# Rearranging the first forty microseconds of a four-layer recurrent kernel on one core

## What is computed

```
h = x_norm @ Win.T + bin
for each of 4 layers:
    y = silu(layernorm(h));  y = sconv(y)      # complex decaying recurrence along the tokens
    h = h + y * scl
    y = silu(layernorm(h) @ W1.T + b1) @ W2.T + b2
    h = h + y
x = x + layernorm(layernorm(h) @ Wout.T + bout)
```

## Time and profile before

| | |
|---|---|
| median of three timed runs | 204.45 us (204.21 to 204.62) |
| profiled execution | 204.57 us, of it the span 202.8 us |
| PE busy | 181.9 us, 90% of the span |
| DVE busy | 157.4 us, 78% |
| ACT, POOL busy | 109.8 us, 84.0 us |
| bytes moved | 15.31 MB, most of them in the first 31 us |

### The profile page before, as it was taken

One profiled execution on the slowest core, in us unless ns is written; L12 is line 12 of the kernel. 1 busy time (PEld: TensorE's weight loads), 2 busy tenths in 40 slices (PEclk: granted clock), 3 DMA queues, 4 the chain that ended last, 5 costly groups with the idle time before them and its releaser, 6 DMA issues.

```text
span 202.8 us, 3759 instructions
## 1 busy us (share of the span) xinstructions
PE 181.9 (90%) x1210; PEld 148.8 (73%) x1210; DVE 157.4 (78%) x547; ACT 109.8 (54%) x281; POOL 84.0 (41%) x142
## 2 busy tenths in 40 slices
PE   0797996859999998999999899999999898988992
PEld 0797995758988788788998689989988444555430
DVE  6898978886588768784977776655899997998872
ACT  1595687524456467637555445462836585863210
POOL 4222269724044422343224522467462735555400
PEclk9999999978999999999999999999999999999999
DMA  5999990000000000000000000000000000002675
GB/s 158 419 376 400 417 368 14 5 0 0 0 5 0 0 3 0 0 3 0 0 0 5 0 0 0 3 0 3 2 0 2 0 3 0 2 0 105 228 283 216
DMA packets 5505, 15.31 MB, mean 75 GB/s; under 512 B 925, under 2 KB 1965, under 8 KB 4462
## 3 DMA queue, kind: packets, MB, share of 16 engines
q1 hardware_dynamic: 5486, 15.07, 19.7%
HBM read 10.87 MB, written 4.19 MB: 74 GB/s over the span
## 4 chain that ended last, share of the span: by engine, by line
PE 68%; DVE 7%; POOL 7%; DMA 6%; ACT 5%; issue 3%; SPq 2%; DVEq 0%; ACTq 0%
PE bank L1508 15%; PE bank L1400 11%; PE bank L1632 7%; PE bank L1490 6%; DMA M<-in_mraw 6%; PE bank L1464 4%; PE bank L1452 4%; POOL RS L360 4%; PE bank L1567 3%; PE bank L1638 3%; POOL M L380 2%; PE bank L1440 2%; PE bank L1556 2%; ACT XA L593 2%; DVE Z L1001 1%
## 5 line engine op out<-in xcount | busy, mean ns | idle before, releaser
L360 POOL TENSOR_TENSOR RS<-SS,nhalf 128x4 f32<-128x4 f32 x36 | 42.9, 1202 | 67.9 <-DVE SS L995 67.6
L1508 PE MATMUL bank<-ffst,HD 128*128 128x128 f32 x256 | 32.7, 283 | 0.0
L1508 PEld LDWEIGHTS bank<-ffst,HD 128*128 128x128 f32 x256 | 31.3, 200 | 0.2
L995 DVE TENSOR_REDUCE SS<-SQ 128x4 f32<-128x260 f32 x36 | 15.2, 421 | 20.9 <-ACT SQ L635 20.3
L1400 PE MATMUL bank<-M,XT 128*128 128x226 f32 x128 | 27.6, 362 | 0.1
L659 ACT ACTIVATE HD<-bank,b1r 128x512 f32<-128x512 f32 x32 | 20.3, 684 | 10.9 <-PE bank L1490 10.8
L1400 PEld LDWEIGHTS bank<-M,XT 128*128 128x128 f32 x128 | 23.2, 189 | 3.6 <-issue 3.1
L635 ACT ACTIVATE SQ<-bank 128x256 f32<-128x256 f32 x36 | 13.8, 383 | 19.6 <-PE bank L1508 9.6
L640 ACT ACTIVATE Y<-bank,cvst 128x512 f32<-128x512 f32 x16 | 12.5, 779 | 15.1 <-PE bank L1452 15.1
L1035 DVE TENSOR_TENSOR_SCAN V<-cvst,U 128x514 f32<-128x514 f32 x16 | 19.5, 1218 | 0.0
L1490 PE MATMUL bank<-Z,w1r 64*128 64x256 f32 x128 | 18.1, 402 | 0.4
(11 more groups left out here) (265 smaller groups left out, 346.0 us busy)
## 6 DMA issues: line engine op xcount, KB each, us to landing
XT<-in_xT SPq DMA_DIRECT2D x4, 1024.0 KB, 11.7
X<-in_x SPq DMA_DIRECT2D x4, 1024.0 KB, 14.0
out<-X SPq DMA_DIRECT2D x8, 512.0 KB, 2.9
w1r<-in_w1d SPq DMA_DIRECT2D x1, 516.0 KB, 16.5
lt<-in_late SPq DMA_DIRECT2D x1, 449.5 KB, 16.3
M<-in_mraw SPq DMA_DIRECT2D x1, 448.0 KB
w2r<-in_w2n SPq DMA_DIRECT2D x1, 256.0 KB, 11.8
winr<-in_win SPq DMA_DIRECT2D x1, 254.0 KB, 2.6
```

What stands on the lines that cost most here:

```text
L360: pool.tensor_tensor(RS[:, g, :], SS[:, g, :], nhalf[:, :], ALU.pow).then_inc(done, 1)
L995: dve.tensor_reduce(SS[:, g, :], SQ[:, g, :, :], AX.X, ALU.add).then_inc(done, 1)
L1508: last = pe.matmul(HK[g][:, j * P:(j + 1) * P], HD[:, u % 2, a, at:at + P], ffst[:, L, a * P:(a + 1) * P], start=False, stop=True, skip_gr ...
```

## The change

Everything in it is an order of work or a wait that follows from one; two things are added. No other arithmetic changes.

1. Added: PE runs 9 matmuls of `ones` by `ones` into a spare bank as soon as `ones` is set, and 3 after the mean of Win. Nothing reads them.
2. SP issues chp first, c6 before the first XT, and w2r behind X of group 2, no longer ahead of M.
3. DVE begins with the polar form (chp) and weaves the rest of it into the preparation of Win.
4. `first_h(0)` follows table level 1, where it followed level 3; levels 2 and 3 and the four levels of layer 0 are spread behind it. All four levels of layer 0, and `first_h(1)`, now stand ahead of `modulate(0)`; `scan(0)` stands behind `sum_squares(1)`, level 4 of layer 1 and `scale_twice(1)`.
5. PE: `turn1(0)` ahead of `mix_columns`; `setup_ffn` behind `column_sums`; `turn1(2)`, `project_x(0)` and `project_x(1)` ahead of `turn2(0)` and `hidden(0)`. The two projections get banks 6 and 7, and `hidden(0)` waits until they are read.
6. ACT and POOL lists of the filling are written out in an order to match. `square(0)` of the second norm stands between tiles 13 and 14 of the squares; on POOL the norm of unit 0's second half stands behind `input_rstd(3)`.
7. The bias of W2 for unit 0 is one float32 matmul of one row, ahead of the products, in place of the split bf16 one behind them. It waits for `b2_mean`; `ffn_splits` moves behind `sum_squares(4)`.
8. `score_rows` is cut in two: two instructions in step 13, the last four (`score_rests`) in step 14, both ahead of that step's `sum_squares`.

The core of the diff:

```
# SP
+ chp; winr; binr; c6; then as before, with w2r behind X of group 2
# POOL
+            def first_steps():
+                norm(0, ss1, rs1)
+                input_rstd(1)
+                norm(1, ss1, rs1)
+                centre_m(0)
+                input_rstd(2)
+                centre_m(1)
+                norm(2, ss1, rs1)
+                centre_m(2)
+                centre_m(3)
+                input_rstd(3)
+                norm(0, ss2, rs2)
+                norm(3, ss1, rs1)
+                norm(1, ss2, rs2)
+                norm(4, ss1, rs1)
+                norm(2, ss2, rs2)
# ACT
+                square(0, (h0_done, 1), sq1)
+                input_mean(1)
+                input_squares(GT, 2 * GT)
+                mix_rows()
+                silu1(0)
+                square(1, (h0_done, 2), sq1)
+                input_mean(2)
+                input_squares(2 * GT, 2 * GT + 2)
+                column_means()
+                input_squares(2 * GT + 2, 3 * GT)
+                silu1(1)
+                ffn_out()
+                square(2, (h0_done, 3), sq1)
+                input_mean(3)
+                input_squares(3 * GT, 3 * GT + 2)
+                square(0, (a1, 1), sq2)
+                input_squares(3 * GT + 2, 4 * GT)
+                silu1(2)
+                x_out(0)
+                square(3, (h0_done, 4), sq1)
+                x_out(1)
+                z_out(0)
+                square(1, (a1, 2), sq2)
+                silu2(0, 0); silu2(0, 1)
+                silu1(3)
+                square(4, (a2, 1), sq1)
+                z_out(1)
...
# DVE, behind input_stats(0)
+                table_level(0, 0, DEPTH)
+                table_level(1, 0, DEPTH)
+                first_h(0)
+                table_level(2, 0, DEPTH)
                 sum_squares(0, sq1, ss1)
+                table_level(3, 0, DEPTH)
                 scale_twice(0)
+                for k in range(4, 8):
+                    table_level(k, 0, 1)
+                first_h(1)
                 modulate(0)
                 sum_squares(1, sq1, ss1)
                 table_level(4, 1, 2)
                 scale_twice(1)
+                scan(0)
+                demodulate(0)
                 modulate(1)
                 first_h(2)
+                sum_squares(2, sq1, ss1)
+                table_level(5, 1, 2)
+                scale_twice(2)
+                scan(1)
+                demodulate(1)
+                sum_squares(0, sq2, ss2)
+                ffn_means()
+                first_h(3)
                 scale(0, rs2, z2)
+                modulate(2)
+                sum_squares(3, sq1, ss1)
+                scale_twice(3)
                 sum_squares(1, sq2, ss2)
+                scan(2)
                 scale(1, rs2, z2)
                 demodulate(2)
                 modulate(3)
                 sum_squares(4, sq1, ss1)
+                ffn_splits()
                 table_level(6, 1, 2)
                 sum_squares(2, sq2, ss2)
...
+                if s == 13:
+                    score_rows()
+                if s == 14:
+                    score_rests()
                 if GROUPS <= s + 1 < STEPS:
                     sum_squares(s + 1, sq1, ss1)
# PE
+            pe.wait_ge(pool_step, 4)
+            warm(9)
...
             last.then_inc(win_mean, 1)
+            warm(3)
...
                 turn1(0)
+                mix_columns()
                 first_h(2)
                 column_sums()
+                setup_ffn()
                 turn1(1)
                 first_h(3)
+                mix_in(0)
+                turn1(2)
+                project_x(0)
+                mix_in(1)
+                project_x(1)
                 turn2(0, 0)
                 hidden(0)
```

More of the change, by code:

```diff
@@ L362, in step @@
             def step(s):
[L363 to L369, removed]
                 if GROUPS <= s + 1 < STEPS:
@@ L495, in mix @@
                 pool.tensor_tensor(out, GX[:, 2:5, a:b], C2[:, :, a:b], ALU.add).then_inc(mix_ready, 1)
-            for s in range(UNITS + 1):
+            first_steps()
+            for s in range(GROUPS, UNITS + 1):
                 step(s)
[L499 to L503, removed]
             cross(0)
@@ L682, in step @@
                     last_z(s)
[L683 to L689, removed]
+                for t in XSTEP.get(s - 1, ()):
+                    x_out(t)
                 if GROUPS <= s + 1 < STEPS:
@@ L850, in link, with mark @@
                 dve.wait_ge(dve_step, chain[0])
+            def mark(ins):
+                chain[0] += 1
+                ins.then_inc(dve_step, 1)
             for q in range(SG):
@@ L1194, in _ @@
             input_stats(0)
-            for k in range(4):
-                table_level(k, 0, DEPTH)
-            first_h(0)
             first_steps()
@@ L1357, in _, with warm @@
         def _(pe):
+            def warm(n):
+                for i in range(n):
+                    pe.matmul(SPARE[:, 0:P], ones[:, :], ones[:, :], start=True, stop=True)
+            pe.wait_ge(pool_step, 4)
+            warm(9)
             pe.wait_ge(pool_step, 9)
@@ L1391, in project_x @@
                 pe.wait_ge(m_done, VC)
-                if t >= 2 and t not in XSECOND:
+                if t < 2:
+                    pe.wait_ge(w2_read, 2)
+                elif t not in XSECOND:
                     pe.wait_ge(xa_read, t)
@@ L1518, in first_steps @@
                 turn1(0)
+                mix_columns()
                 first_h(2)
                 column_sums()
-                mix_in(0)
+                setup_ffn()
                 turn1(1)
                 first_h(3)
+                mix_in(0)
[3 more added lines that the diff above has]
+                project_x(1)
                 turn2(0, 0)
-                mix_in(1)
-                turn1(2)
                 hidden(0)
-                for t in XSTEP[2]:
-                    project_x(t)
             def step(s):
@@ L1648, in _ @@
             first_h(1)
-            mix_columns()
-            setup_ffn()
             first_steps()
```

105 lines of the change are left out of this document (42 added, 63 removed).

## The result

| | before | after |
|---|---|---|
| median of 20 runs each, on one chip | 204.47 us (from 203.32) | 203.75 us (from 201.59) |
| ratio after to before | | 0.9949 [0.9927, 0.9970] |
| profiled execution, of it the span | 204.57, 202.8 us | 203.30, 201.5 us |

The change gains 0.7 us in the median, and 1.0 us by the ratio, where 3.3 were forecast.

What follows compares the result with a forecast made beforehand. PE was taken as the bound behind the filling, so `turn1(4)`'s start decides. Filling -2.2 us (1.3 + 1.84 - 0.8, less 0.15) and score rows -1.1 make -3.3: 201.3 profiled, 201.1 median; likeliest 200.4 to 202.0, overall 199.9 to 203.3.

Steps and rivals of the forecast that it cites:

- The sum: Whole kernel: 2.2 us from the filling and 1.1 from the score rows, 3.3 us less in all.
- So I take the clock as high, gain 1.84.: End of the filling on PE: no empty stretch like 40:42 remains, so the clock stays high, gaining 1.84 us.
- rival A: New filling: the clock falls again in new PE gaps, one fall costing about 1.84 us, giving 203.0; chance 0.2.
- M and XT of group 2 come 0.63 us earlier: Load queue: with w2r behind X of group 2, these loads come 0.63 us earlier, XT landing at 20.3.
- `first_h(0)`, `scale_twice(0)`, the first products: Early filling: `first_h(0)` at 14.27 (was 16.03), `scale_twice(0)` at 17.55 (was 19.30), 32 product instructions in about 3.8 us.
- all the early gains end in a tie: PE to 32 us: work ends at 31.95, about 31.7 before, since the loads and `setup_ffn` take the early gains.
- `turn1(3)` at 41.35: Late filling on PE: `turn1(3)` starts at 41.35 in place of 42.65, a gain of 1.3 us.
- Rival C: Second half of unit 0 becomes the bound, deciding from `scale(0)` at 39.0; slower beyond 42.3, 204.8; chance 0.08.
- Step 3: Behind `turn1(3)`: the norm beside `scan(2)` takes 1.87 us, leaving 0.8 us new idle time; `hidden(1)` at 45.75, before 47.94.
- Score rows: Steps 13 and 14: splitting the six instructions lets them fit DVE's idle time, gaining 1.11 us, 0.8 if they overrun.
- Rival D: Warming raises nothing, the clock falls at 40 as before, only score rows and 0.9 remain: 203.4; chance 0.1.
- Rival B: Norms are quicker, unit 1's falling ahead of the scan for 0.8 us less, and DVE doesn't hold: 200.1; chance 0.1.

Runs made afterwards that it cites:

- e1: The changed kernel plus 8 reader-less matmuls ahead of `turn1(0)` and 4 ahead of `first_h(2)`: 201.70 us, 0.9886 of before.
- e11: e7 with 1 in place of 4 reader-less matmuls ahead of `first_h(2)`: 201.34 us, 0.9851 of before.
- e4: The kernel before plus 10 reader-less matmuls behind the two projections of x, in the gap ahead of `turn1(3)`: 202.79 us, 0.9955 of before.
- e3: The kernel before with only the score rows split over steps 13 and 14: 201.92 us, 0.9898 of before.
- e10: The same kernel as e3, run again: 202.97 us in the median of 12, 0.9923 of before.
- e8: e2 without its first 9 and 3 reader-less matmuls: 202.96 us in the median of six, 0.9884 of before.
- e2: e1 plus reader-less matmuls ahead of `turn1(2)` (4) and around `hidden(0)` (2 and 2): 201.78 us, 0.9893 of before.
- e5: e3 plus reader-less matmuls, 3 ahead of `turn2(0)` and 10 behind the projections of x (old order of the filling): 201.94 us, 0.9865 of before.
- e9: e6 with the f32 bias row of unit 0 moved from the head of `project(0)` to the gap ahead of `hidden(0)`: 200.93 us, 0.9840 of before.
- e6: e2 with the sum of squares of unit 1's second half moved ahead of `scale_twice(3)` on DVE: 201.78 us, 0.9854 of before.
- e12: e11 with the sum of squares moved as in e6 and the bias row as in e9: 200.33 us, 0.9805 of before.
- e7: e2 with the first loads issued in the old order, w2r still behind X of group 2: 201.83 us, 0.9857 of before.

## Why the prediction was wrong, point by point

**The sum.** It said 3.3 us; the profiled executions differ by 204.57 - 203.30 = 1.27. Of the missing 2.0 the clock is 1.6 (e1) and the late load about 0.4 (e11). The forecast of `turn1(4)` says the same: 50.05 forecast, 52.02 as built, 50.43 in e1, 49.96 in e11.

**The step that failed: "So I take the clock as high, gain 1.84."** The old fall did go, and its price was nearly right (1.58 by e4, and by e3 against e10; the 1.84 took 52.26 of the chain for the start of `turn1(4)`, and with the 52.10 of the timeline the same difference is 1.68). What I had not carried through was the other side. I listed the gaps of 16.3 to 18.3 and 19.9 to 20.3 under rival A and set them aside because "in each, PE works more than in 39.9 to 42.65". That compares single gaps. Together with the transposes and small products between them they make 4.5 us with 1.52 of PE work, more idle time than the 2.76 us that brought the clock down before. The stretch should have been judged as a whole; then A, at 0.2, would have been the likeliest case. Its time, 203.0, is what the 0.992 group after shows (202.63 to 203.30).

**The second mistake of that step: treating the fall as certain.** One profile of before showed it, and I took the whole 1.84 as there in every execution. e3 and e10 show that the same gap costs it in some and not in others; the table of runs shows both kernels doing so. Nine of after's 20 executions have a still lower clock, 0.979 to 0.983, and 0.4 to 1.4 us more. No profile of after caught one of them. The one of e8 shows that a second fall can lie at 177 us, for 0.01 of the mean clock and 1.2 us, which fits in size; that it is the same fall is not shown. It would also fit the single executions at 0.988 or 0.989 in e2, e5 and e9, each 1.0 to 1.1 us above its neighbours. In e1 none came in 6 runs.

**"M and XT of group 2 come 0.63 us earlier": failed.** XT landed at 20.93, where the old figure was 6.42 + 14.5 = 20.92. I took w2r off the queue's account and left out what chp and c6, which the same edit puts ahead, do to the stream behind them: XT of group 0 is issued at 2.69, before at 2.10, and the first slice of the page moves at 112 GB/s, before at 158. e11 takes them back and has the load 0.4 us earlier, with 0.44 us in the time (against e2, and part of that may be the shorter `warm` there). In the five profiles of the old loads the landing scatters from 20.4 to 21.2, so the direction of the w2r step looks right, and its size, 0.4 at most, is not measured well.

**`first_h(0)`, `scale_twice(0)`, the first products: right.** 14.46, 17.74 and 3.84 us, forecast 14.27, 17.55 and 3.75 to 3.8. But the forecast's own remark that "all the early gains end in a tie" is what e5 measures: with the clock held, the new order of the filling and the old one are 0.16 us apart in time.

**`turn1(3)` at 41.35: right with the clock held** (41.79 in e1, 41.65 in e2, 41.32 in e11), 43.38 as built. `scan(0)` came at 25.57 (25.7), `scale(0)` at 40.16 for 38.1; in e2, at the high clock, it is 38.43. Rival C had its point of decision at 39.0: 40.16 is beyond it, by the clock and not by DVE, and the cost seen, 1.6 us, is that of the clock alone. From `turn1(3)` to `turn1(4)` it is 8.64 us after and 8.63 in e2: the whole step moved with `scale(0)`, and C's mechanism did not decide.

**Step 3: right size, with one of two causes missed.** `turn1(3)` to `hidden(1)` was forecast as 41.35 to 45.75, 4.40 us; e1 has 41.79 to 46.20, 4.41. I put 0.8 us on the norm beside the scan and 0.15 on "rounding and the f32 bias row". The norm did take 1.86 us (forecast 1.87), and it does hold `mix_in(2)` up: DVE is ready for it 3.26 us behind `turn1(3)` in e2 (44.91 - 41.65), forecast 3.45. By the Trainium skill's page "SBUF — State Buffer", section "Who interferes with whom", a VectorE instruction with two SBUF inputs contends with a GpSimd instruction that reads SBUF, and the one that issues later waits. The 1.86 us begin at 43.74, inside the scan of 43.57, and agree. What the forecast missed is the second wait at the same place. The f32 bias row costs 0.62 us from its start to the next one (43.97 to 44.59 after), and it stands on the path because the new order brings `project(0)` to where PE has no gap. With it PE takes 3.3 us from `turn1(3)` to `mix_in(2)` even with the early norm (41.87 to 45.19 in e6), as much as in e2. So e6, which makes that norm 1.0, wins 0.1 us, and e9, which moves the bias row as well, wins 0.83 more. That the sum came right in spite of a term put at next to nothing is luck: the two costs ran side by side. The old order takes a bf16 row there, 0.11 us to the next start (50.72 to 50.83 for the same line in e2).

**Score rows: right.** 1.11 us forecast, and 7.35 - 6.24 = 1.11 measured; no sum of squares in steps 13 and 14 starts late. It is the one part of the change that gains its full price without help.

**Rival D** (nothing but the score rows and 0.9) gave 203.4, near the measured 203.75, but by another mechanism: the warming does make the first products quick and the old fall does go. **Rival B** needed norms ahead of the scan; e6 gave it one, and it was worth 0.1 us, not 0.8, as long as the bias row stood in its place. With both away (e9, e12) the 0.93 us came, and e12's 200.33 is close to B's 200.1.

## What to carry to other kernels

When you close a gap that costs the clock, look for the stretches that the new order thins out, and judge each as a whole, with the small matmuls in it; a few matmuls that nobody reads, in the gap and ending before the next work is ready, were worth more here (1.3 to 2.05 us) than the whole new order as built (0.2 to 0.4). A fall of the clock seen in one profile may be there in some of the executions only: read the granted clock of every run before you count on its price. And ask of each small instruction on the path what it costs at its precision: the one-row f32 pair was 0.6 us. Where two waits end at one place, as this pair and the norm did, an experiment that removes one of them shows next to nothing (0.1 us in e6) and says nothing of what both are worth (0.93).

## What the runs showed of the hardware that was not expected

- Whether the granted clock falls differs from one execution to the next: the same program with the same 2.76 us gap had 1.00 in 44:46 in one profiled execution and 0.50 in another (e3, e10), for 1.58 us.
- It also falls behind a stretch in which PE is not idle throughout but works 1.52 of 4.5 us (after; e1, with the gaps filled, kept it), and once behind one in which it worked 2.26 of 3 us (e8, 174 to 177 us; e2, with 2.25 of 3, kept it).
- The contention of DVE and POOL goes both ways. `scan(1)` after takes 1.70 us beside `centre_m` (1.34 for two pieces), where a scan takes 1.22; `centre_m` had taken 1.66 beside a scan before and takes 0.80 alone.
- An f32 matmul with one row and 256 columns costs 0.31 us an instruction on PE, two of them 0.62; the bf16 one that does the same work in later steps takes about 0.11 to the next start.
- Where two small transfers (chp, 14 KB, and c6, 12.5 KB) are issued ahead of the stream, the first slice of the page moves at 92 to 114 GB/s (six profiles), where they are not, at 134 to 167 (e7, e11, e12); the third 1 MB load of XT then lands some 0.3 us later in the median, with a scatter nearly as large.
